# Perceiver layer with a mixture of experts: the gathered expert rows are scaled before they are stored and added into x by the gathers themselves

## What is computed

```python
scores = jax.nn.softmax(logits, axis=-1)
_, topk_ids = jax.lax.top_k(scores, NUM_EXPERTS_PER_TOK)        # 2 of 8
w = scores * in_topk
h = jax.nn.silu(g) * u
expert_out = jnp.einsum('nei,ehi->neh', h, experts_down)
out = jnp.einsum('neh,ne->nh', expert_out, w)
out = out + shared_weight * shared
x = x + out
```

## Time and profile before

| | |
|---|---|
| time, median of 3 runs | 700.09 us (700.0 to 700.1) |
| the profiled execution's own time | 699.82 us |
| its span, first to last instruction | 697.9 us |
| granted TensorE clock | 1.00 of full speed |
| TensorE busy | 689.1 us |
| VectorE busy | 557.0 us |
| ScalarE busy | 339.3 us |
| GpSimd busy | 208.4 us |

### The profile page before, as it was taken

The page is one execution under the profiler, slowest core; times in us unless marked ns, Lnnn a source line. Parts: engine busy times, 40 slices in busy tenths (PEclk is TensorE's granted clock), DMA queues, the critical chain, the costliest instruction groups (busy, mean ns, idle before and its releaser), DMA issues.

```text
span 697.9 us, 9865 instructions
## 1 busy us (share of the span) xinstructions
PE 689.1 (99%) x3197; PEld 568.6 (81%) x3197; DVE 557.0 (80%) x713; ACT 339.3 (49%) x454; POOL 208.4 (30%) x154
## 2 busy tenths in 40 slices
PE   8999999999999999999999999999999999999996
PEld 7788888887888788888888888878888888888884
DVE  5688788888989998899996753769434799899896
ACT  4322222222245565556663333642233588888872
POOL 5844545444430000000000001226784111211254
PEclk9999999999999999999999999999999999999999
DMA  8057666767742236432210612514200799999974
GB/s 303 16 169 216 220 228 235 244 228 235 236 140 91 92 120 272 152 116 92 90 60 0 239 48 76 231 58 165 91 1 2 290 353 387 383 410 362 414 275 149
DMA packets 38974, 130.70 MB, mean 187 GB/s; under 512 B 6690, under 2 KB 10788, under 8 KB 35876
## 3 DMA queue, kind: packets, MB, share of 16 engines
q1 hardware_dynamic: 36548, 124.72, 49.6%
q0 software_dynamic: 1536, 4.20, 1.9%
q10 hardware_dynamic: 864, 1.44, 0.6%
HBM read 120.89 MB, written 9.46 MB: 187 GB/s over the span
## 4 chain that ended last, share of the span: by engine, by line
PE 95%; issue 1%; DVE 1%; POOL 1%; DMA 1%; ACT 0%; DVEq 0%; POOLq 0%
PE ps L1041 25%; PE ps L991 8%; PE ps L992 8%; PE ps L995 8%; PE ps L1265 5%; PE ps L883 4%; PE ps L885 4%; PE ps L884 4%; PE ps L1235 4%; PE ps L1246 3%; PE ps L1244 3%; PE ps L1245 3%; PE ps L899 2%; PE ps L946 2%; PE ps L1168 1%
## 5 line engine op out<-in xcount | busy, mean ns | idle before, releaser
L461 POOL TENSOR_TENSOR c_lo<-ring,c_hi 128x512 fp32r<-128x512 f32 x64 | 85.0, 1329 | 90.1 <-ACT c_hi L608 90.1
L608 ACT ACTIVATE c_hi<-ring 128x512 fp32r<-128x512 f32 x64 | 40.4, 634 | 128.4 <-PE ps L995 111.8
L478 POOL TENSOR_TENSOR w_lo<-raw,w_hi 128x1024 fp32r<-128x1024 f32 x11 | 26.7, 2432 | 250.7 <-ACT w_hi L727 236.7
L991 PE MATMUL ps<-qk_hi,c_hi 128*128 128x512 f32 x256 | 100.7, 393 | 0.0
L992 PE MATMUL ps<-qk_lo,c_hi 128*128 128x512 f32 x256 | 99.7, 389 | 0.0
L1471 DVE TENSOR_TENSOR runmax<-runmax,att 128x512 f32<-128x512 f32 x64 | 93.9, 1466 | 3.9
L995 PE MATMUL ps<-qk_hi,c_lo 128*128 128x512 f32 x256 | 68.6, 389 | 0.0
L1041 PE MATMUL ps<-p_hi,d_hi 128*128 128x512 f32 x256 | 64.2, 393 | 0.1
L1465 DVE SCALAR_TENSOR_TENSOR att<-ring,beta,ps 128x512 f32 (+1 forms) x64 | 47.8, 747 | 20.7 <-PE ps L995 20.1
L1041 PE MATMUL ps<-p_hi,d_lo 128*128 128x512 f32 x256 | 63.3, 389 | 0.0
L1041 PE MATMUL ps<-p_lo,d_hi 128*128 128x512 f32 x256 | 63.2, 389 | 0.0
(11 more groups left out here) (324 smaller groups left out, 1506.1 us busy)
## 6 DMA issues: line engine op xcount, KB each, us to landing
ring<-stream SPq DMA_DIRECT2D x64, 512.0 KB, 3.5
raw_u<-up_in SPq DMA_DIRECT2D x22, 1024.0 KB, 6.9
raw_d<-down_in SPq DMA_DIRECT2D x33, 512.0 KB, 7.0
ring<-ctx_in SPq DMA_DIRECT2D x32, 512.0 KB, 3.3
raw<-shared_in SPq DMA_DIRECT2D x11, 768.0 KB, 6.0
raw_u<-up_last_in SPq DMA_DIRECT2D x11, 768.0 KB, 6.7
slots<-blank SPq DMA_DIRECT2D x15, 256.0 KB
late<-wqkv_in SPq DMA_DIRECT2D x1, 3072.0 KB, 10.7
```

The costliest lines, as they stand in the source:

```text
L461: pool.tensor_tensor(c_lo[:, s % 2, :], ring1[:, s, 0, :], c_hi[:, s % 2, :].bitcast(F32), ALU.subtract).then_inc(lo1_ready, 1)
L608: act.activation(c_hi[:, s % 2, :], ring1[:, s, 0, :], ACT.Copy).then_inc(hi1_ready, 1)
L991: pe.matmul(ps[:, s, :], hi, qk_hi[:, k, :], start=(k == 0), stop=False)
```

## The change

- `keep` scales: the copy of PSUM bank 2 to `y_out` takes the tokens' weights as its scale, a column of `info_all` addressed by the unit's register. ScalarE waits for `info_full` before unit 0.
- The eight gathers write into `x` with an add in the DMA, in place of a copy to `met`. The four tiles of choice 0 are gathered first, two counted by `met_first`, two by `met_second`. Before it issues those of choice 1 for the same tiles, GpSimd waits until they have landed. GpSimd also waits for the shared expert's additions before the first gather.
- `add_met`, ScalarE's two scalings and GpSimd's two additions are removed, and the tile `met` with them.
- VectorE waits, before its final additions, for `met_full` (now choice 1, tiles 0 and 1) and before that of tile 2 for `met_rest`. The numbers at which the stores wait for `added` are lower by the six additions that are gone.

```diff
@@ sync
             for st in range(0, ST, 2):
-                sp.wait_ge(added, 2 * ST + 2 + st + 1)
+                sp.wait_ge(added, ST + st + 1)
                 sp.dma_start(out[st * P:(st + 1) * P, :], x[:, st, :]).then_inc(out_stored, 16)
...
@@ gpsimd
             def gather_kept(c, first, last, landed):
                 for st in range(first, last):
-                    pool.indirect_dma_start(met[:, c, st, :], None, slots,
-                                            bass.IndirectOffsetOnAxis(kept_of[:, c, st:st + 1], 0)).then_inc(landed, 16)
+                    pool.indirect_dma_start(x[:, st, :], None, slots,
+                                            bass.IndirectOffsetOnAxis(kept_of[:, c, st:st + 1], 0),
+                                            compute_op=ALU.add).then_inc(landed, 16)
...
-            gather_kept(0, 0, ST, met_full)
-            gather_kept(1, 0, 2, met_second)
+            pool.wait_ge(added, ST)
+            gather_kept(0, 0, 2, met_first)
+            gather_kept(0, 2, ST, met_second)
+            pool.wait_ge(met_first, 16 * 2)
+            gather_kept(1, 0, 2, met_full)
+            pool.wait_ge(met_second, 16 * 2)
             gather_kept(1, 2, ST, met_rest)
-            pool.wait_ge(added, 2 * ST)
-            for st in range(2, ST):
-                pool.wait_ge(met_step, st - 1)
-                pool.tensor_tensor(x[:, st, :], x[:, st, :], met[:, 1, st, :], ALU.add).then_inc(met_added, 1)
@@ scalar
-                act.activation(y_out[:, :], ps[:, 2, :], ACT.Copy).then_inc(y_ready, 1)
+                act.activation(y_out[:, :], ps[:, 2, :], ACT.Copy,
+                               scale=info_all[:, bass.ds(u, 1), 1:2].rearrange("p a c -> p (a c)")).then_inc(y_ready, 1)
...
+            act.wait_ge(info_full, 16)
             unit(0, first=True)
...
-            act.wait_ge(met_rest, 16 * (ST - 2))
-            for st in range(ST // 2, ST):
-                act.activation(met[:, 1, st, :], met[:, 1, st, :], ACT.Copy, scale=weight_of[:, 1, st:st + 1]).then_inc(met_step, 1)
...
@@ vector
-            def add_met(c, first, last):
-                if c == 0:
-                    dve.wait_ge(met_full, 16 * ST)
-                else:
-                    dve.wait_ge(met_second, 16 * 2)
-                dve.wait_ge(added, ST * (c + 1))
-                for st in range(first, last):
-                    dve.scalar_tensor_tensor(out=x[:, st, :], in0=met[:, c, st, :], scalar=weight_of[:, c, st:st + 1],
-                                             in1=x[:, st, :], op0=ALU.mult, op1=ALU.add).then_inc(added, 1)
-
...
                                       ALU.subtract).then_inc(dn_last_ready, 1)
-                    add_met(0, 0, 2)
                 product_e(u, 2)
...
-                    add_met(0, 2, ST)
                     hidden_low(u, 2, last)
                     read_info(u)
                     way_back(1)
-                    add_met(1, 0, 2)
                     output_low(1)
...
-            dve.wait_ge(added, 2 * ST + 2)
+            dve.wait_ge(added, ST)
+            dve.wait_ge(met_full, 16 * 2)
             for st in range(ST):
                 dve.wait_ge(out_psum, st + 1)
-                if st >= 2:
-                    dve.wait_ge(met_added, st - 1)
+                if st == 2:
+                    dve.wait_ge(met_rest, 16 * 2)
```

More of the change, by code:

```diff
@@ L177, in perceiver_layer @@
         y_out = at("y_out", [P, D], F32, 172)
-        met = at("met", [P, 2, ST, D], F32, 152)
         back = at("back", [P, S], F32R, 178)
@@ L276, in perceiver_layer @@
         y_ready, y_stored = sem("y_ready"), sem("y_stored")
-        met_full, met_second, met_rest = sem("met_full"), sem("met_second"), sem("met_rest")
+        met_first, met_second = sem("met_first"), sem("met_second")
+        met_full, met_rest = sem("met_full"), sem("met_rest")
         turned_psum, xg_hi_ready, xg_lo_ready = sem("turned_psum"), sem("xg_hi_ready"), sem("xg_lo_ready")
@@ L281, in perceiver_layer @@
         y_psum_e, y_hi_ready, y_lo_ready, scattered = sem("y_psum_e"), sem("y_hi_ready"), sem("y_lo_ready"), sem("scattered")
-        out_psum, added, met_step, met_added = sem("out_psum"), sem("added"), sem("met_step"), sem("met_added")
+        out_psum, added = sem("out_psum"), sem("added")
         down_hi_ready, down_lo_ready = sem("down_hi_ready"), sem("down_lo_ready")
@@ L415, in _ @@
             for st in range(0, ST, 2):
-                sp.wait_ge(added, 2 * ST + 2 + st + 1)
+                sp.wait_ge(added, ST + st + 1)
                 sp.dma_start(out[st * P:(st + 1) * P, :], x[:, st, :]).then_inc(out_stored, 16)
-            sp.wait_ge(added, 2 * ST + 2 + 5)
+            sp.wait_ge(added, ST + 5)
             sp.dma_start(out[3 * P:S, D // 2:D], x[:, 3, D // 2:D]).then_inc(out_stored, 16)
@@ L849, in _ @@
             unit(final, last=True)
-            act.wait_ge(met_rest, 16 * (ST - 2))
-            for st in range(ST // 2, ST):
-                act.activation(met[:, 1, st, :], met[:, 1, st, :], ACT.Copy, scale=weight_of[:, 1, st:st + 1]).then_inc(met_step, 1)
-            act.wait_ge(added, 2 * ST + 2 + 2)
+            act.wait_ge(added, ST + 2)
             act.dma_start(out[P:2 * P, :], x[:, 1, :]).then_inc(out_stored, 16)
-            act.wait_ge(added, 2 * ST + 2 + 4)
+            act.wait_ge(added, ST + 4)
             act.dma_start(out[3 * P:S, 0:D // 2], x[:, 3, 0:D // 2]).then_inc(out_stored, 16)
```

## The result

The changed kernel takes **701.36 us** (median; 700.35 to 703.54), the one before 699.99 (699.58 to 700.21) beside it: ratio 1.0021 [1.0015, 1.0027], 1.4 us slower. Forecast was 698.2, faster by 1.9 us, in a range of 697.9 to 703.0: the time lies in the range, on the other side of no change. The profiled execution took 700.69 us, span 698.7, against 699.82 and 697.9 before: +0.87 us. The last unit lies 0.15 us later than before (GpSimd's first gather starts at 673.02 and 672.87, ScalarE's SiLU at 684.00 and 683.85), so that much is to be taken off when they are laid beside the earlier trace rows.

A forecast was written before the change was run, and what follows sets the result against it. TensorE, busy 99% of the 697.9 us span, was taken as the bound, so only its waits could give time. Closing two (1.76 + 0.16 = 1.92 us), all other terms 0, gave 700.09 - 1.92 = 698.2 us, range 697.9 to 703.0.

The forecast's parts named there:

- Moved off VectorE: Last unit: without the additions of met before the third product, TensorE's waits of 1.76 and 0.16 us close, 1.92 us gained.
- Removed: Last unit: two ScalarE scalings and two GpSimd additions (2.52 us for the pair) go; they held nobody, worth nothing.
- the scale in keep: ScalarE's copy to y_out in each unit: up to 0.2 us more, nine times, 1.8 us if unhidden; taken as hidden, 0.
- GpSimd's two waits: Before the fifth and seventh gathers, for earlier gathers to land: cost nothing at copy speed.
- The formula of the landing: Eighth gather lands at the later of 676.25 + 8s and 682.5 + 5s, plus 0.4 us; full gain up to 691.9.
- s: What one adding gather costs the DMA engines when gathers queue: taken as 1.7 us, between 1.34 and 2.34.
- rival B: DMA engines in the last unit: the second reads queue, s from 1.9 to 2.33, time 698.7 to 701.5 us; chance 0.18.
- the queue's start: First burst of the last unit's gathers on the DMA engines, kept at 676.25 us as in the kernel before.
- rival C: GpSimd writes more for each adding gather, 1.4 or 1.9 us against 0.95: 698.4 to 704.2 us; chance 0.12.
- Rival D: DMA engines become the bound, an adding gather costing twice a copy, s = 2.7 us: 704.4 us, slower; chance 0.26.
- E: TensorE waits in the last unit for something other than the additions, so nothing changes: 700.1 us; chance 0.04.
- A: The forecast itself: s up to 1.9, GpSimd near 0.95 us per gather, 698.2 us (698.0 to 698.7); chance 0.40.

The follow-up runs named there:

- the second trace: The changed kernel measured once more, with nothing altered: 701.21 us, ratio 1.0015 to the kernel before.
- the first trace: The profiled execution of the changed kernel in its first measurement: 700.69 us, where the median was 701.36 us.
- no_chain: Changed kernel, but choice 1's gathers add into a cleared tile of their own, so GpSimd skips both waits for choice 0's landing: 700.59 us, ratio 1.0013.

## Why the prediction was wrong

**Moved off VectorE: right.** 1.92 us worked out, 1.99 measured with copying gathers; the transposes start at 685.40 - 0.15 = 685.25, forecast 685.26.

**Removed, and the scale in keep: right.** Nothing and nothing; ScalarE took 0.155 us more for a unit, under the 0.2 allowed, and the kernel with the scale alone lost nothing. One bound was too tight: I had the last store of kept rows landed by 672.5 "at the latest"; in the second trace it landed at 672.96 and GpSimd waited 0.30 us for it. GpSimd's two waits: nearly right, 0.40 us at the seventh gather in the first trace and 1.05 in the second, and without them (no_chain) the last gather landed no earlier than in the first.

**The formula of the landing: right.** Start of the first burst, plus 8 s, plus 0.4, with s the time that one gather costs in the engines' queue. What went into it was wrong, in two places.

**The step that failed is s**, taken as 1.7 us out of 1.34 to 2.34. I let the second read cost 0.68 us of engine work, from the row scatter's stretch, and let it fill the idle share. Measured is 1.88 in place of 1.54 for the work, a doubling of the copy and not an addition of a cheaper read, and 0.88 in place of 0.90 for the share that a full queue reaches. 1.88 / 0.88 = 2.14. The divisor was good. The dividend came from a scatter, in which nothing is added up; why its work is no measure for that of adding is not shown. That s is rival B's (2.15, time 700.1).

The 1.34 us that I took for a copy in a full queue was not a price of the engines either. GpSimd made the last copies 1.25 and 1.34 us apart (684.10, 685.35 and 686.69, of which the earlier trace rows shows the last two), and the engines' share was 0.64: they got no more to do. No run shows copies in a full queue.

**The second wrong term is the queue's start.** I kept 676.25; it was 677.0. The first gather is stretched beside VectorE and took 3.53 us, 2.89 before: 0.64 of the 0.75. That is about what GpSimd's own work on a gather grew by, from the 0.95 that I kept to 1.54. That is rival C's mechanism. With full rows it acts through this start alone, as the queue never runs dry after it; with half rows, where it does, it cost 0.52 us. So 677.0 - 0.15 + 17.3 + 0.4 = 694.6 on the axis of before, where 693.8 meant no change: +0.8, and +0.87 was measured on the profiled executions. The 17.3 is 8 times the 2.17 that was read from the landing, so this sum had to come out; with the 2.13 of the rate, which is independent of it, it is +0.5 from 677.0 and +0.7 from 677.25. The medians differ by 1.4. The remaining 0.5 is of the size by which the second trace, at the median, lands later than the first (0.7 us); its cause is open.

**Rival D.** Its premise came true and its time did not. By the rows, the engines' work on a gather doubled (0.91 to 1.88), but its time in the queue went from 1.34 to 2.17, 1.6 times, as the copies had left a third of the engines idle. The Trainium skill (Collectives: The Full Stack, "The bandwidth ceiling: the fold count and why AG ≠ RS ≠ AR") gives, for the reduce-scatter of a ring, half the rate for two source reads; the doubled work agrees with it, the measured rate of 123 against 196 GB/s, a factor of 0.63, does not, as the copies were not bound by the engines. E falls: TensorE's holes closed.

The right reading of the same rows would have been to multiply the copy's engine work by two (0.86 x 2 = 1.72) and divide it by the full queue's 0.9, 1.9 us: the edge between A and B, still under the 2.17 found.

## What to carry to other kernels

An accumulation in a DMA is not free work taken off an engine: here it doubled the DMA engines' work for its bytes and lengthened GpSimd's by 0.6 us for 128 rows. So count the gathers that fit into the slack and let only those add (two here, the first ones). The gain sat in the order on one engine and could be had by moving the additions behind what TensorE needs. A rate read from a queue is the engines' price only where their share is near 1; at 0.64 it was the pace of whoever fed them. When work is spread over VectorE and GpSimd, additions of two SBUF tiles should not run side by side on both.

## What the hardware showed that was not expected

- An adding gather of 128 rows of 2 KB: 1.54 us on GpSimd at its shortest (copy 0.95; 1.54 with half rows too), 1.88 us of full DMA engines (copy 0.91; adding half rows 0.97), 64 packets more at either row size, 123 GB/s at a share of 0.88 (copies 196 at 0.64), 5.6 to 6.0 us from issue to landing in after (copies in before 3.6 to 3.8).
- VectorE's addition of two SBUF tiles took 0.68 us alone and up to 3.41 beside GpSimd's, and GpSimd's 2.65 us of additions took 3.02, 3.12 and 3.79.
- One of GpSimd's first two instructions of the last unit is stretched beside VectorE's long subtraction (2.29 us): in some executions the one-column addition, from 0.2 to between 2.1 and 2.4 us, in others the first gather, to 2.9 us (copy) or 3.5 to 3.6 (adding).
